# Selected columns in two PSUM banks, with one-hots made column by column

## What is computed

```python
h = jnp.maximum(_layernorm(x, axis=-1), 0.0)
# the layer, on h:
rol, col = (edge_index[0], edge_index[1])            # source, destination
e_feat = jnp.concatenate([x[rol], x[col], edge_attr], axis=-1)
h = jax.nn.relu(e_feat @ W1 + b1)                     # 96 -> 64
v = h @ W2 + b2                                       # 64 -> 32
x_cand = jax.ops.segment_max(v, col, num_segments=num_nodes)
return jnp.maximum(x_cand, x[:, -v.shape[-1]:])       # added to x outside
```

## Time and profile before

| | before |
|---|---|
| median of 3 runs | 4758.86 us (4730.09 to 4797.8) |
| profiled execution | 4765.93 us |
| its span | 4764.1 us |
| granted TensorE clock, mean | 0.801 |
| instructions | 41821 |

### The profile page before, as it was taken

The page is one execution under the profiler, slowest core; times in us unless marked ns, Lnnn a source line. Parts: engine busy times, 40 slices in busy tenths (PEclk is TensorE's granted clock), DMA queues, the critical chain, the costliest instruction groups (busy, mean ns, idle before and its releaser), DMA issues.

```text
span 4764.1 us, 41821 instructions
## 1 busy us (share of the span) xinstructions
PE 2960.5 (62%) x11492; PEld 2111.3 (44%) x11492; DVE 2078.8 (44%) x3562; ACT 748.1 (16%) x1058; POOL 2733.4 (57%) x2852
## 2 busy tenths in 40 slices
PE   1266566567676666666666666565766656565677
PEld 0144344445454444444444444444544444444445
DVE  5044344444444444444444444343444434444447
ACT  3011111111111111111111111111111111111111
POOL 6456555556665556565566556555655555565550
PEclk8578778788787878887888887778878888787788
DMA  4322222222222222222222222222222222221222
GB/s 99 76 58 53 46 54 47 52 49 59 49 53 47 56 50 55 50 54 47 53 51 51 54 49 51 51 47 52 55 48 50 47 53 51 49 58 43 53 52 44
DMA packets 245595, 252.33 MB, mean 53 GB/s; under 512 B 83265, under 2 KB 199479, under 8 KB 239113
## 3 DMA queue, kind: packets, MB, share of 16 engines
q10 hardware_dynamic: 20790, 103.55, 9.1%
q1 hardware_dynamic: 133938, 101.54, 7.4%
q0 software_dynamic: 90784, 46.48, 7.1%
HBM read 239.86 MB, written 11.52 MB: 53 GB/s over the span
## 4 chain that ended last, share of the span: by engine, by line
another core or an unknown queue 44%; PE 21%; DVE 15%; issue 14%; DVEq 3%; ACT 3%; ACTq 1%; SPq 0%; DMA 0%; POOL 0%; POOLq 0%
PE ps_spare L570 11%; DVE sel_tmp L958 3%; DVE running L929 3%; DVE best L995 3%; PE ps_turned L603 2%; DVE key_hot L947 2%; DVEq L989 2%; PE ps_hid L582 2%; PE ps_val L591 1%; PE ps_feat L537 1%; PE ps_hid L580 1%; DVE edge_hot L940 1%; PE ps_picked L612 1%; DVE feat L965 1%
## 5 line engine op out<-in xcount | busy, mean ns | idle before, releaser
L480 POOL DMA_INDIRECT feat<-h_rows,idx x2821 | 2716.6, 963 | 1900.3 <-issue 993.3
L570 PE MATMUL ps_spare<-table,key_hot 128*128 128x448 f32 x5642 | 1500.6, 426 | 395.6 <-DVE sel_tmp L958 348.0
L570 PEld LDWEIGHTS ps_spare<-table,key_hot 128*128 128x128 f32 x5642 | 1259.8, 230 | 524.3 <-DVE sel_tmp L958 339.0
L958 DVE SCALAR_TENSOR_TENSOR sel_tmp<-off_place,offset,ps_spare 128x448 f32<-128x448 f32 x403 | 273.6, 679 | 1553.4 <-remote 1234.1
L603 PE MATMUL ps_turned<-ident,running 128*128 128x128 f32 x806 | 171.9, 351 | 939.4 <-DVE running L929 733.7
L722 ACT ACTIVATE hidden<-ps_hid,b_col 128x1024 f32<-128x1024 f32 x202 | 224.8, 1113 | 2681.5 <-remote 2196.6
L603 PEld LDWEIGHTS ps_turned<-ident,running 128*128 128x128 f32 x806 | 116.2, 175 | 1088.5 <-DVE running L929 805.1
L980 DVE TENSOR_TENSOR ends<-ps_turned,ends 128x512 fp32r<-128x512 f32 x202 | 139.5, 690 | 786.4 <-ACT ends L734 579.8
L995 DVE TENSOR_TENSOR best<-ps_picked,best 32x64 f32 x1612 | 355.0, 220 | 162.9 <-remote 96.6
L947 DVE TENSOR_TENSOR key_hot<-dst_rows,ps_iota 128x1792 fp32r<-128x1792 f32 x202 | 406.1, 2011 | 18.1 <-DMA dst_rows<-key_rows 18.1
L580 PE MATMUL ps_hid<-feat_t,w_blk 128*128 128x512 f32 x806 | 413.8, 595 | 0.0
(11 more groups left out here) (125 smaller groups left out, 893.7 us busy)
## 6 DMA issues: line engine op xcount, KB each, us to landing
dst_rows<-loc_rows ACTq DMA_DIRECT2D x98, 512.0 KB
feat_t<-attr_rows_in ACTq DMA_DIRECT2D x98, 512.0 KB
feat<-h_rows,idx POOLq DMA_INDIRECT x2821
dst_rows<-key_rows SPq DMA_DIRECT2D x101, 256.0 KB
term_ring<-term_rows SPq DMA_DIRECT2D x404, 64.0 KB
dst_rows<-keep_rows SPq DMA_DIRECT2D x100, 256.0 KB
term_rows<-best SPq DMA_DIRECT2D x3, 1792.0 KB
idx<-src_cols_in SPq DMA_DIRECT2D x51, 32.0 KB
```

What stands on the lines that cost most here:

```text
L480: nc.gpsimd.indirect_dma_start(feat[:, slot, k, :], None, h_dram, bass.IndirectOffsetOnAxis(ap=idx[:, c % IDX, k:k + 1].bitcast(U32), axis=0),
L570: mm = pe.matmul(ps_sel, key_hot[:, c // TWO % 2, g, P * (c % TWO):P * (c % TWO) + P], table[half][:, g, :], start=(g == 0 and half == 0), ...
L958: nc.vector.scalar_tensor_tensor(out=sel_tmp[:].rearrange("p (f a) -> p f a", a=SA), in0=off_place[:].unsqueeze(1).broadcast_to([P, D, SA] ...
```

## The change

The work on the numbers stays: two columns a pair are selected, by the same matmuls, and GpSimd makes the same gathers. The diff does five things.

1. `select` writes the even columns into `ps_spare0` and the odd ones into `ps_spare1`, and waits for `sel_step` of the column before the last. Columns are numbered j, with `SEL` = 2 a pair, and `take_selected` waits for its own `sel_ready` of the column before.
2. `place_keys` makes the one-hot of one column (128x896), into one of four slots (`HOTS`), four columns ahead. It is called at the end of each `take_selected`, so twice a turn; before it stood once a turn between the first take and `keep_best`.
3. `turn_ends` and `pick_ends` write the same bank, `ps_turned`, which frees the bank that (1) needs. `turn_ends` waits for a new semaphore `best_taken`, raised by `keep_best` of the pair before. In the preparation the third bank of `end_bank` is now `ps_hid`'s second.
4. The four staging tiles of the preparation move into `x_even`, whose refill (`win_dmas` of x) waits for them, and whose first contents must have been read (`cent_done`) before they are loaded. `term_ring` and `key_ring` change places in memory.
5. The keys in DRAM are numbered by column (404 rows, before 408), and the loads of four keys have the same size as before.

```diff
@@ SyncE @@
             def load_key(s, half):
-                sp.dma_start(key_ring[:, FOUR * half:FOUR * half + FOUR, :].rearrange("p c e -> p (c e)"),
-                             key_dram[bass.ds(s, FOUR), :].rearrange("c e -> (c e)").unsqueeze(0)
-                             .broadcast_to([P, FOUR * P])).then_inc(s_key[half], 16)
+                lo, n = half * 2 * SEL, 2 * SEL
+                sp.dma_start(key_ring[:, lo:lo + n, :].rearrange("p c e -> p (c e)"),
+                             key_dram[bass.ds(s, n), :].rearrange("c e -> (c e)").unsqueeze(0)
+                             .broadcast_to([P, n * P])).then_inc(s_key[half], 16)
...
+            sp.wait_ge(S["cent_done"], 2)
             sp.wait_ge(S["key_pad"], 1)
...
+            sp.wait_ge(S["key_out"], 16 * NSB)
+            sp.wait_ge(S["off_step"], 5)
             win_dmas(sp.dma_start, x, x_even, False, 0, T, S["x_win_in"])
...
             def group(i, g):
                 if is_chunk(i, FOUR * g + 3 * FOUR):
-                    sp.wait_ge(S["hots_made"], i * UNROLL + 2 * g + 4)
-                    load_key(i * (UNROLL * 2) + FOUR * g + 3 * FOUR, (g + 1) % 2)
+                    sp.wait_ge(S["hots_made"], i * (UNROLL * SEL) + 2 * SEL * (g + 2))
+                    load_key(i * (UNROLL * SEL) + 2 * SEL * (g + 3), (g + 1) % 2)
@@ TensorE @@
-            def select(i, c):
-                pe.wait_ge(S["hots_made"], i * UP + c // TWO + 1)
-                if not known(i) or c > 0:
-                    pe.wait_ge(S["sel_step"], i * UNROLL + c)
+            def select(i, j):
+                pe.wait_ge(S["hots_made"], i * (SEL * UP) + j + 1)
+                if not known(i) or j > 1:
+                    pe.wait_ge(S["sel_step"], i * (SEL * UP) + j - 1)
                 for g in range(SG):
                     for half in range(2):
-                        mm = pe.matmul(ps_sel, key_hot[:, c // TWO % 2, g, P * (c % TWO):P * (c % TWO) + P],
-                                       table[half][:, g, :], start=(g == 0 and half == 0),
-                                       stop=(g == SG - 1 and half == 1))
+                        mm = pe.matmul(ps_sel[j % 2], key_hot[:, j % HOTS, g, :], table[half][:, g, :],
+                                       start=(g == 0 and half == 0), stop=(g == SG - 1 and half == 1))
                 mm.then_inc(S["sel_sum"], 1)
...
             def turn_ends(i, v):
-                if not later(i, v):
+                if later(i, v):
+                    pe.wait_ge(S["best_taken"], i * UP + v)
+                else:
                     pe.wait_ge(S["check_step"], 7)
                 pe.wait_ge(S["run_ready"], i * UP + v + 1)
@@ VectorE @@
-            def take_selected(i, c):
-                if known(i) and c % TWO:
-                    dve.wait_ge(S["sel_ready"], c)
-                dve.wait_ge(S["sel_sum"], i * UNROLL + c + 1)
+            def take_selected(i, j):
+                c, k = column(j)
+                if not known(i) or j > 0:
+                    dve.wait_ge(S["sel_ready"], i * (SEL * UP) + j)
+                dve.wait_ge(S["sel_sum"], i * (SEL * UP) + j + 1)
...
+                if is_column(i, j + HOTS):
+                    place_keys(i, j + HOTS)
...
-                if is_chunk(i, TWO * v + 2):
-                    take_selected(i, TWO * v + 2)
-                if is_chunk(i, TWO * v + 4):
-                    place_keys(i, v + 2)
+                for j in ahead[0:1]:
+                    take_selected(i, j)
                 if later(i, v - 1):
                     keep_best(i, v - 2)
-                if is_chunk(i, TWO * v + 3):
-                    take_selected(i, TWO * v + 3)
+                for j in ahead[1:2]:
+                    take_selected(i, j)
```

More of the change, by code:

```diff
@@ L25 @@
 PRE = 5
-GK = COLS - 1
+SEL = 2
+HOTS = 4
 SA = 14
@@ L169, in gnn_layer @@
         ps_turned = pb("ps_turned")
-        ps_picked = pb("ps_picked")
         ps_iota = pb("ps_iota")
-        ps_spare = pb("ps_spare")
+        ps_spare = [pb(f"ps_spare{n}") for n in range(2)]
+        ps_picked = ps_turned
         ps_flag = ps_turned[:, 2 * P:3 * P]
-        ps_sel = ps_spare[:, 0:SN]
-        ps_made = [ps_val, ps_spare]
-        end_bank = [ps_feat[:], ps_hid[:, 0, :], ps_turned[:], ps_picked[:]]
+        ps_sel = [bank[:, 0:SN] for bank in ps_spare]
+        ps_made = [ps_val, ps_spare[0]]
+        end_bank = [ps_feat[:], ps_hid[:, 0, :], ps_hid[:, 1, :], ps_turned[:]]
         ps_place = ps_iota[:, 0:WIN]
@@ L221, in gnn_layer @@
         LOOPS = (NP - PRE) // UP
-        TURN = 16 * GK
         def known(s):
@@ L249, in is_chunk, with is_column, column @@
             return not known(i) or c < C
+        def is_column(i, j):
+            return not known(i) or j < SEL * (NP - 1) + 1
+        def column(j):
+            return j, COLS - 1
         def load_rows(eng, s, half, count):
@@ L367, in _ @@
             sp.wait_ge(S["key_made"], 1)
-            for b in range(-(-CPAD // P)):
-                r = min(P, CPAD - b * P)
+            for b in range(NSB):
+                r = min(P, NSEL - b * P)
                 sp.dma_start(key_dram[b * P:b * P + r, :], key_stage[0:r, b, :]).then_inc(S["key_out"], 16)
@@ L478, in step @@
                 pool.sem_inc(S["chunk_begun"], 1)
-                for k in range(GK):
+                for k in range(COLS - 1):
                     nc.gpsimd.indirect_dma_start(
@@ L617, in step @@
             def step(i, v):
+                ahead = [j for j in range(SEL * v + SEL, SEL * v + 2 * SEL) if is_column(i, j)]
                 if later(i, v):
@@ L638, in _ @@
             pe.wait_ge(S["table_ready"], 2)
-            for c in range(TWO):
-                select(0, c)
+            for j in range(SEL):
+                select(0, j)
             steps(pe, step, {1: turn_worst})
@@ L997, in keep_best @@
                         mm.then_inc(S["best_half"], 1)
-                if known(i) and v == NP - 1:
-                    mm.then_inc(S["best_done"], 1)
+                mm.then_inc(S["best_done" if known(i) and v == NP - 1 else "best_taken"], 1)
             def step(i, v):
+                ahead = [j for j in range(SEL * v + SEL, SEL * v + 2 * SEL) if is_column(i, j)]
                 if later(i, v - 1):
@@ L1028, in _ @@
             dve.wait_ge(S["firsts_in"], 16)
-            for v in range(2):
-                place_keys(0, v)
-            for c in range(TWO):
-                take_selected(0, c)
+            for j in range(HOTS):
+                place_keys(0, j)
+            for j in range(SEL):
+                take_selected(0, j)
             steps(dve, step, {1: check})
```

79 lines of the change are left out of this document (41 added, 38 removed).

## The result

The changed kernel takes **4984.1 us** (median of 4 runs, 4962.55 to 4991.5) beside 4756.03 us of the kernel before: ratio 1.0463, 95% interval 1.0381 to 1.0546. It is slower, and outside the forecast's range. The profiled execution has a span of 4989.7 us, 225.6 us over the 4764.1 us of before. On the chip of e17 to e19 the kernel before ran at two levels, 4815.47 and 4831.95 us and three times 4892 to 4903 us; the two faster runs (median 4823.71 us) are the measure there, and by all five (median 4891.89 us) the 5.9% of e19 would be 4.5%.

A forecast was written before the change was run, and what follows sets the result against it. No engine is full; a circle of waits between GpSimd, TensorE and VectorE bounds the kernel. Terms -12, -14, +67 and -27 give +14 on 4765.93, so 4780 us profiled; median forecast 4775 us, range 4600 to 4900 us.

The forecast's parts named there:

- The circle: Engines wait on each other: second take, scan, transposes, next gathers; GpSimd waits for the transposes 82 times, 626.6 us.
- The second bank: Second selection no longer waits for the first take: 44 waits, 348.0 us, to fall under 60, little of it gained.
- The terms of 12 and 14 us: Second bank's gains: 1.2 us in each of ten late-take turns, 3.4 us in each of four held turns.
- the held turns: Nine turns with the second selection pushed into the next gather burst, its signal coming at burst end; four won back.
- One-hots by column: A 1.0 us one-hot now stands between second take and scan, making 2.25 us instead of 1.25; +67 us.
- the spare 8 us: Slack of the serial path in turns that GpSimd paces, said to hide the one-hot there; cost 0.
- the count of 68 turns: Turns paying the exposed one-hot: 82 waiting for the path less ten late and four held; 0.98 us each, +67 us.
- the 27 us got back from groups of turns: A held turn saved spares part of the long-gap group behind it; -54 us at most, half taken, -27.
- rival (1): Exposed one-hot between second take and scan is paid in all 202 turns: +198 us, 4957 us; chance 0.25.
- The wait added for `sel_ready`: VectorE's wait for its own semaphore before a take, said to be met a take earlier; cost 0.
- The shared bank: `turn_ends` on TensorE waits for `best_taken`, with 9 us of cover, so never the last wait; cost 0.
- SyncE and preparation: Key loads half a turn earlier: 0, up to 1 us in 50 turns; key rows after centring: 0, bound 5 us once.

The follow-up runs named there:

- e17: Kernel before with four of seven gathers left out per chunk from the 17th on, plus VectorE's wait for its own `sel_ready`; 3061.43 us, late signals.
- e19: The changed kernel unaltered, with all gathers, measured a third time; 5110.32 us beside 4823.71 us of the kernel before, on a chip with late signals.
- e16: Kernel before with two selection banks and the shared bank alone, four gathers a chunk left out; 2719.73 us, chip without late signals.
- e18: e16 with VectorE's wait for `sel_ready` taken out inside the loop; 2983.61 us, on a chip with late signals.
- e4: The changed kernel with both one-hots made behind the first take; 3656.71 us beside 3651.57 us of the kernel before, no late signals.
- e1: Kernel before with only the banks changed (two selection banks, shared bank); 3652.83 us beside 3651.57 us of the kernel before, no late signals.
- e3: Kernel before with only the one-hots made by column, the second behind the second take; 3652.66 us beside 3651.57 us, no late signals.
- e6: The changed kernel unaltered, measured again; 5003.38 us beside 4741.98 us of the kernel before, ratio 1.0561, on a chip with late signals.
- e13: Kernel before with three gathers instead of seven for each chunk from the 17th on; 2639.49 us, chip without late signals.

## Why the prediction was wrong

**The circle** was read rightly for the long gaps: the path from the second take through scan and transposes to the next gathers, entered when the selection's signal comes. That the selection's end and its signal differ was right as well. What the reading lacked is that the feature transposes' own signal is late in the short gaps.

**The second bank.** The forecast said that the 348.0 us go (they did, and under 60 us was right) and that little of it is gained. With fewer gathers its worth is about nothing: 1.2 us of cost by e16 to e18, if the two chips can be put together. In the first pair of profiles the second take comes 18.15 instead of 18.48 us after the feature transposes (means of 184 turns), 0.33 us earlier, at most 61 us in all. The terms of 12 and 14 us lie between the two and were not measured by themselves. The 14 us had a misreading under them: both idle times shown for the held turns, 4.64 and 6.86 us in the earlier trace rows, ended with "issue" and are not among the 44 waits. The Trainium skill, TensorE: Matmul & The Clock Gate, section "HAM oscillation — how this bites in real kernels", tells of a kernel that gained nothing more from PSUM double-buffering. The 1.2 us agree with it.

**One-hots by column.** Size right (1078 ns, 2.24 us from take to scan), place right. The step that failed is this one: "In the turns that GpSimd paces it lies in the spare 8 us: 0." With it stood the count of 68 turns and the 27 us got back from groups of turns. The forecast has no row for the 8 us. In the traces the turns with a short gap had 5.8 us in hand on average, 27 of the 120 had under 1.5, and the serial part grew by 1.45 us a turn. 30 gaps more became long, and that is worth 178 us; in the 90 short ones that were left 2.8 us were in hand. The longer path and the groups pulled the same way, and the forecast had given the groups the other sign.

That is rival (1), "the path's spare is eaten by late signals"; it had a chance of 0.25. Counted by turns it holds too: the mean turn grew from 22.68 to 23.80 us, by 1.12, which is 1.45 of longer path less the 0.33 above, so on average nearly every turn pays. That its 4957 us lie only 27 us under the measured median is in part luck. Its sum has 0.98 us a turn for the one-hot alone, without the loop's start, the slower transposes and the 0.33 us back.

**The wait added for `sel_ready`** was costed at 0 as "met a take earlier". As a wait it is met. As an instruction, with the eight more of the one-hots, it lengthened VectorE's loop, and with the longer loop came the idle time at its start: 32.6 us in 23 turns in the changed kernel. With fewer gathers, where TensorE's clock fell behind half of these stalls too, one instruction was 79 us. No term of the sum had it.

**The transposes were slower.** From the ends' transposes to the end of the feature transposes it is 1.87 us on average instead of 1.51. TensorE's granted clock is 0.792 over the run instead of 0.801; how much of the 0.36 us is the clock was not worked out. Per turn the serial part from second take on grew by 1.45 us: 1.00 one-hot, 0.18 loop start, 0.36 slower transposes, less 0.09 between scan and transposes. The forecast had 0.98.

**The shared bank**: cost 0, right as far as e18 shows.

**SyncE and preparation**: no wait for keys within the loop. With fewer gathers the first scan came 25 us later (187.8 against 162.8 us): VectorE waited for keys once more, 29.4 us, ahead of a one-hot at 177.7 us. The bound of 5 us was too small there. In the first pair the wait for keys is 19.1 against 18.1 us, the first scan is 18.4 us later for a reason not shown, and the eleventh scan stands at 507.6 against 509.2 us, so nothing of it is left.

**The signs.** GpSimd's wait of 8.01 us each lay in the 8.0 to 8.6 forecast, the count (107 for "down by ten or so" from 82) did not, and the text had named that count as the one to watch.

**What stays open.** How the 178 us split between the one-hot's place, the loop's start and the bank under late signals was not measured: e4, e1 and e3 never met such a chip. Of the 230 us more in the gaps 90 lie in the 23 turns at the loop's start (10.25 instead of 6.33 us each), where the path is longer by 1.4 us of stall and 1.0 of one-hot; from that the shares can't be told apart. Whether two banks with early one-hots and a loop of the old length would beat the kernel before there is open too; e18 on such a chip shows only that it is 2.5% faster than one bank with the longer loop. Why some chips have late signals isn't known.

## What to carry to other kernels

Price a step by whether it stands between a signal that comes late and the work that starts the next round. Where turns are of two kinds, an average of spare time is no cover: count the turns that have less in hand than the edit adds, and price a change of kind for each. When an edit lengthens an unrolled loop, look at the instruction queue's packets and at idle time with the releaser "issue" behind the branch: a wait that never has to wait can still cost. And before explaining a wait as the kernel's, see whether another chip has it.

## What the hardware showed

- **Late signals on some chips.** On two of the seven chips of the experiments TensorE's semaphore updates come late when raised over 6 us into a burst of indirect gathers: 98% of those 6 to 18 us in (e6), by 4 to 9.5 us on average in the first measurement's trace. On the five others none of over 1400 in each trace is late. The kernel before takes 4742 and 4824 us on the two and 3651 to 3660 us on the others, 30 to 32% apart. With bursts of six gathers (e18) 191 of 192 signals raised 6 to 10 us in are late as well, but by 1.7 us on average.
- **One instruction.** With fewer gathers and 325 instructions between branches on VectorE the instruction queue had 16 packets in the whole run (e13, e18); with 326 there were 115 more in 23 trips (e16, e17), and VectorE stood 2.7 to 3.0 us behind the branch (0.24 us with 325).
- **The clock follows, sometimes.** After 2.01 us of idle time TensorE's granted clock stood at 0.55 for 3 us, and the fourteen matmuls of a selection took 4.52 us instead of 3.08. Idle times of 2.0 to 2.4 us stood at all 23 loop starts of e16, and the clock fell behind 12 of them.
